# A decoder kernel on one core: GpSimd pauses twice in its hand-ordered summation chain

## The reference

```python
x = x + L0_attn(layernorm(x))          # delta-rule attention, 2 heads, chunks of 64
x = x + L0_xattn(layernorm(x), ctx)    # 16 heads, tanh layers on q, k, v
x = x + L0_ffn(layernorm(x))           # router, top 2 of 4 experts, hidden 512
x = x + L1_attn(layernorm(x))          # causal, shared key and value, 16 heads
x = x + L1_xattn(layernorm(x), ctx)    # causal, 16 heads
x = x + L1_ffn(layernorm(x))           # top 2 of 8 experts, hidden 128
```

## Time and profile before

| | us |
|---|---|
| median of 3 runs (5360.71 to 5361.69) | 5361.09 |
| profiled execution | 5361.46 |
| its span, first to last instruction | 5359.7 |
| PE busy | 4697.3 (88%) |
| PEld busy | 3072.0 (57%) |
| DVE busy | 4119.1 (77%) |
| ACT busy | 2322.5 (43%) |
| POOL busy | 3977.9 (74%) |

### The profile page before, as it was taken

The page is one execution under the profiler, slowest core; times in us unless marked ns, Lnnn a source line. Parts: engine busy times, 40 slices in busy tenths (PEclk is TensorE's granted clock), DMA queues, the critical chain, the costliest instruction groups (busy, mean ns, idle before and its releaser), DMA issues.

```text
span 5359.7 us, 108430 instructions
## 1 busy us (share of the span) xinstructions
PE 4697.3 (88%) x28362; PEld 3072.0 (57%) x28362; DVE 4119.1 (77%) x11313; ACT 2322.5 (43%) x4480; POOL 3977.9 (74%) x12365
## 2 busy tenths in 40 slices
PE   1089999999999999999999999999999999899989
PEld 0065656656565565656556565665656556565655
DVE  8867777777777877787777777777777777777778
ACT  0044444454444444443454544445444444444444
POOL 6688585868858587785858868586895858678585
PEclk7599999999999999999999999999999999999999
DMA  3000000000000000000000000000000000000000
GB/s 90 12 9 9 21 1 25 5 9 21 9 21 1 25 5 9 21 1 29 1 13 17 9 21 1 25 5 9 21 9 21 1 25 6 9 21 6 17 1 17
DMA packets 61911, 78.34 MB, mean 15 GB/s; under 512 B 11168, under 2 KB 53808, under 8 KB 61232
## 3 DMA queue, kind: packets, MB, share of 16 engines
q1 hardware_dynamic: 52784, 62.42, 3.5%
q10 hardware_dynamic: 8448, 8.39, 0.5%
HBM read 45.04 MB, written 8.46 MB: 10 GB/s over the span
## 4 chain that ended last, share of the span: by engine, by line
PE 62%; DVE 22%; issue 8%; ACT 6%; SPq 1%; POOL 1%; DVEq 0%; DMA 0%; ACTq 0%; POOLq 0%
PE bank L1264 7%; PE bank L1297 5%; PE bank L1357 5%; PE bank L1183 5%; PE bank L1169 4%; PE bank L1383 3%; PE bank L1195 3%; PE bank L1217 3%; PE bank L1093 3%; DVE smax L1890 3%; PE bank L1100 3%; DVE arena L1500 2%; PE bank L1282 2%; ACT arena L856 2%; PE bank L1175 2%
## 5 line engine op out<-in xcount | busy, mean ns | idle before, releaser
L1890 DVE TENSOR_REDUCE smax<-bank 128x4 f32<-128x512 f32 x768 | 525.4, 684 | 82.8 <-PE bank L1175 37.7
L843 ACT ACTIVATE arena<-bank 128x512 f32<-128x512 f32 x768 | 455.1, 593 | 249.9 <-PE bank L1183 244.1
L1894 DVE TENSOR_TENSOR arena<-bank,smax 128x512 f32<-128x512 f32 x768 | 531.2, 692 | 26.5
L509 POOL TENSOR_TENSOR arena<-arena 128x1024 f32<-128x1024 f32 x17 | 32.2, 1893 | 664.8 <-DVE y_nat L1622 664.7
L1183 PE MATMUL bank<-ident,arena 128*128 128x128 f32 x3072 | 485.5, 281 | 42.3 <-ACT arena L830 25.0
L1264 PE MATMUL bank<-w,arena 128*128 128x512 f32 x1024 | 498.6, 619 | 14.0 <-DVE arena L1832 14.0
L1169 PE MATMUL bank<-arena 64*128 64x512 f32 x1536 | 441.1, 651 | 64.4 <-ACT arena L867 28.0
L1183 PEld LDWEIGHTS bank<-ident,arena 128*128 128x128 f32 x3072 | 346.6, 141 | 242.9 <-ACT arena L832 82.2
L1297 PE MATMUL bank<-w,arena 128*128 128x256 f32 x2048 | 454.1, 380 | 13.9 <-ACT arena L902 13.9
L830 ACT ACTIVATE arena<-arena,rstd 128x512 f32<-128x512 f32 x512 | 368.2, 719 | 199.9 <-DVE arena L1894 195.8
L648 POOL TENSOR_TENSOR acc_a<-acc_s,arena 128x32 f32<-128x32 f32 x1008 | 273.2, 271 | 225.9 <-DVE gate L2011 103.5
(11 more groups left out here) (437 smaller groups left out, 11925.4 us busy)
## 6 DMA issues: line engine op xcount, KB each, us to landing
arena<-in_x_dram SPq DMA_DIRECT2D x35, 512.0 KB, 3.6
xn_next<-arena SPq DMA_DIRECT2D x17, 512.0 KB, 2.9
arena<-cum_dram SPq DMA_DIRECT2D x17, 512.0 KB, 3.8
arena<-in_ctx_dram SPq DMA_DIRECT2D x16, 512.0 KB, 4.0
out_dram<-arena ACTq DMA_DIRECT2D x16, 512.0 KB, 3.2
xn<-xn_next SPq DMA_DIRECT2D x15, 512.0 KB, 2.9
w<-in_L_ffn_w_dram SPq DMA_DIRECT2D x8, 512.0 KB
w<-in_L_ffn_w_dram SPq DMA_DIRECT2D x1, 1024.0 KB
```

The lines of the kernel that those rows point to most:

```text
L509: operation(*operands).then_inc(sum_step, 1)
L843: act.activation(PT[:, v % 2], bank[3 + v % 2][:, :].rearrange("p (h q) -> p h q", h=QH), ACT.Copy).then_inc(S["pt"], 1)
L1890: dve.tensor_reduce(smax[:, u, :], sc, AX, ALU.max).then_inc(S["s_max"], 1)
L1894: dve.tensor_tensor(Ssb[:, u % 4], sc, smax[:, u, :].unsqueeze(2).broadcast_to([P, QH, P]), ALU.subtract).then_inc(S["s_sub"], 1)
```

## The change

GpSimd's chain had one group of rounds from 25 to 58, and now has three, with a wait ahead of round 27 for the norm's step 39 of this iteration (25 steps of `exact_root_seed` and `exact_root`, 6 of the first quotient, 8 remainders), and a wait ahead of round 42 for `k_rows`. The wait for `x_norm` ahead of round 58 is as it was. The assertion on `run["ref"]` only checks the count while the program is built.

```diff
                 pool.wait_ge(S["g_w"], at(it, "g_w", 1))
-                rounds(ROUTER_ROUND, READ_ROUND)
+                rounds(ROUTER_ROUND, QUOTIENT_ROUND)
+                pool.wait_ge(ref_step, nth(it, REF_STEPS, REF_BEFORE + REST_STEPS))
+                rounds(QUOTIENT_ROUND, MIXED_ROUND)
+                pool.wait_ge(S["k_rows"], at(it, "k_rows", 1))
+                rounds(MIXED_ROUND, READ_ROUND)
                 pool.wait_ge(x_norm, nth(it, 1, 1, 2))
@@
                         for part in range(4):
                             for b in range(2):
                                 exact_rest(0, part, b)
+                        assert run["ref"] == REST_STEPS, run["ref"]
                         key_limit(it, 1)
@@
 ROUTER_ROUND = 25
+QUOTIENT_ROUND = 27
+MIXED_ROUND = 42
 READ_ROUND = 58
+REST_STEPS = 39
```

## The result

The changed kernel took 5394.49 us in the median of six executions (5384.93 to 5410.39) against 5360.9 of the kernel before: a ratio of 1.0066, 95% interval 1.0055 to 1.0077. Forecast were 5354.5 with a range of 5338 to 5371. So it is slower by 34 us, and 23 above the range. One of the six executions of the kernel before took 5819.93 us and counts as slow; the ratio leaves it out. One thing belongs to the result at once: the changed kernel's time is not one number. In a later set of executions, beside others on one chip, its median was 5373.66 (5359.61 to 5395.43, eleven executions; ratio 1.0029, 1.0018 to 1.0039), while the kernel before stayed between 5357.5 and 5364.1 in 25 executions there. The experiments show which iterations are hit in an execution, though not why these. What is said of "after" rests on the first set's profile, with a span of 5391.4.

The account below looks back on a forecast made before the run. The path was taken to run from TensorE through VectorE's remainders back to TensorE, GpSimd's own time being no bound. Per iteration -0.91 + 0.5 = -0.41, times 16 -6.6, giving a median of 5354.5 us, range 5338 to 5371.

Parts of the forecast that it names:

- The gain at the remainders: VectorE's first quotient and eight remainders, freed of GpSimd's company, go from 7.54 to 6.63 us: 0.91 gained per iteration.
- TensorE's cover: TensorE's wait of 1.06 us at expert 2's transposes can take in the 0.91; no more than some 1.06 gainable there.
- The pause and the slip: GpSimd pauses 10.5 us ahead of round 27; its chain ends 8.1 later; au keeps a margin of 3.7, no stall.
- The second wait: GpSimd's wait for the key rows ahead of round 42 is satisfied 3.5 us before it is reached: cost 0.
- What slides in beside VectorE: GpSimd's later centering runs beside VectorE's small steps of the decay's exponential: loss 0.5 to 0.8 per iteration, 0.5 taken.
- rival 2: Chain over 9.3 us late, so the centering's subtraction holds an exponential instruction: +0.85 per iteration, 5375 us; chance 0.13.
- The price of a hold: A small VectorE instruction beside GpSimd's subtraction loses at most 1.35 us, bounded by L1788; 0.1 to 0.4 taken.
- No row shows these steps beside GpSimd: Claim that no profile row had the exponential's small VectorE steps beside GpSimd work, so their loss was estimated from other lines.
- The clock adds no term: TensorE's granted clock is 1.00 (2.4 GHz) in the changed stretch and none of its instructions moves: no cost.
- the +-0.3 of the phase: Allowance in the forecast's own range, 5345 to 5366, for how GpSimd's later rounds meet VectorE's instructions.
- The net -0.41: Sum per iteration: 0.91 gained at the remainders less 0.5 lost beside the exponential; times 16, -6.6 us.
- None of the four: Rivals: kinder phase (chance 0.36), centering holds the exponential (0.13), au too late (0.03), pause does nothing (0.06).

Follow-up runs that it names:

- idle_wait: Changed kernel with its wait for the key rows ahead of round 42 replaced by one for a semaphore satisfied long before; 5370.4 us, ratio 1.0024.
- fill_held: Changed kernel with more TensorE filler products, whose results are unused, in the waits around the latent layer; 5367.9 us, ratio 1.0016.
- held_in_four: Changed kernel without the key-rows wait, with added filler products around the latent layer and GpSimd's centering subtraction cut in four; 5359.2 us, ratio 0.9997.
- second_only: Kernel before plus only the wait for the key rows ahead of round 42, without the pause ahead of round 27; 5410.4 us, ratio 1.0092.

## Why the prediction was wrong, by its steps

**The gain at the remainders: right.** 4.13 for the eight, 6.62 for the stretch against 6.63. By expert 2's layer it is 1.55 (26.48 to 24.93), more than forecast, since small collisions vanished as well: L1643, now L1647, is back at 0.17 from 0.42. TensorE's cover was 1.06 as said: the fillers behind the mixture start 1.06 earlier (56.06 to 55.0 after the gates), and the rest waits again, 1.87 instead of 1.32.

**The pause and the slip: right.** 10.3 for 10.5, 8.3 for 8.1. au is in time, and nothing waits for it.

**The second wait: right,** with 2.2 to spare instead of 3.5; idle_wait, with the same time, bears out that it costs nothing.

**What slides in beside VectorE: the mechanism seen, its size wrong.** The loss at the exponential was taken as 0.5 and measured 1.34 in the mean. It was rival 2, with a chance of 0.13, that named such a hold, and it came in 12 of 16 iterations, but by another way than rival 2 said: the chain was 8.3 late and not 9.3, and the instruction held is one of the first or second group, as VectorE was late; only two iterations have it in the third group. Two errors lie in it. The price of a hold was bounded by 1.35 from a line beside a 2.35 addition, and in the sum taken as 0.1 to 0.4; it is 1.64. The 1.35 is no bound. VectorE's timeline before has that line here:
```profile
1655.38 1.51 DVE L1788 TENSOR_TENSOR parts<-hrs 128x4 f32<-128x4 f32 x1
```
It ends at 1656.89, with the addition (1654.53 + 2.35), so the line lasted for what was left of the addition, 1.50, and the 1.35 is that less its own time: the row shows a hold to the end. Nor does L1424 speak for instructions that stay free: in each of its 32 executions less than 0.1 us was left of the instruction that GpSimd was at when it started. A nearer row was in the trace of before, in the prologue, where the very same steps run beside the very same subtraction on GpSimd (timelines of VectorE and GpSimd before):
```profile
238.66 1.82 DVE L1540 COPY dec_t<-a_row 128x2 f32<-128x2 f32 x1
...
240.72 1.74 DVE L1543 TENSOR_SCALAR dec_t<-dec_t 128x10 f32<-128x10 f32 x1
```
```profile
238.56 1.89 POOL L509 TENSOR_TENSOR arena<-arena,row 128x1024 f32<-128x1024 f32 x1
240.53 1.90 POOL L509 TENSOR_TENSOR arena<-arena 128x1024 f32<-128x1024 f32 x1
```
"No row shows these steps beside GpSimd" was false: the line's maximum of 1743 ns beside a median of 173 would have shown it. The other error is the phase. The subtraction came 143.9 us after round 25 (1810.26 less 1666.41), where 143.6 was forecast. VectorE's second group was forecast 0.91 earlier than before, 142.2 after round 25, and came at 144.0, 0.1 after the subtraction. The clock's loss of 1.6 at the latent layer had put it there. So the two causes are linked: the fall pushed the exponential onto the subtraction. fill_held bears this out, where without the fall the second group is past in time.

**"The clock adds no term": this step failed.** It was argued from the stretch that gets faster, where the granted clock is 1.00, and not from the places behind it where TensorE's waits lie and where the clock already falls in the kernel before, two or three times an iteration. There the shift decides. It costs 1.3 at the latent layer and some 0.4 more in the second attention, averaged over the iterations. Pairs on one chip show it as a cause: the fillers take 12 us back (5379.8 to 5367.9, 5371.0 to 5359.2) and leave the kernel before as it is; and a delay of 1.6 makes a loss of 42 without the change, and of 13 with the fillers.

**Two terms that the sum left out.** It let the 0.91 pass on in full and gave the second attention nothing beyond the +-0.3 of the phase. Of 1.57 won by expert 2's layer, held_in_four, without the latent fall and the long hold, has 1.21 left behind the mixture and 0.76 behind the second attention. The net -0.41 an iteration that was forecast would thus not have come without the clock's fall either: at part 9 it is -0.10, in fill_held 0.00.

**The rivals.** None of the four is what happened: rival 2 had half of it. That the range did not reach far enough has one main reason: each mechanism was priced by itself, and none allowed that a shift could set off another loss larger than itself.

**What stays open.** Why the clock falls in this iteration and not in the next, and so how the loss of 13 to 34 us is made up in each execution. Why a delay of 0.75 vanishes in the kernel before is only half answered: the length of the iteration goes with the interval of the falls, but what makes it keep to that is not shown. Nor is it known which came first in the changed kernel, the fall or the hold: its first iteration has the fall without a long hold, but so has that of the kernel before. And why the second attention is 0.5 longer behind the pause.

## What to carry to other kernels

Where TensorE's granted clock falls somewhere in every iteration, times of edits need not add: before pricing an edit by its own stretch, list all the falls and the waits ahead of them, and reckon with a shift of one or two us moving them. Here removing falls with filler products was worth more (29 and 38 us) than the 15 us that the change itself could have brought. Follow a gain from one fixed point to the next before asking where it went: this one was spent before the next gates. A long instruction of GpSimd costs by what it lands on: look for the longest execution of each neighbouring line, the prologue's too, and cut such an instruction in pieces rather than move it.

## What the runs showed of the hardware

- A small VectorE instruction that starts 0.09 or 0.11 us after a GpSimd subtraction of 1.89 us is held to its end: 1.83 for 0.16 (second_only) and 1.80 for 0.16 (after). Cut into four pieces of 0.61 the whole stretch is 0.8 shorter.
- The granted clock falls to 1.2 GHz behind idle times of TensorE of 1.87 and 1.08 close together in the kernel after, and also behind 1.32 and 1.08, which in the kernel before usually bring no fall: the latent product 3.43 in second_only, 1.95 before. The two waits alone do not decide.
- A delay of up to 0.75 us an iteration cost nothing over 16 iterations (5360.1 against 5360.2), one of 1.6 to 1.7 cost 2.6 each.
- The granted clock's falls at the second gates return after 317.44 us in all 15 intervals of four kernels with different edits, and after 320.85 in all 15 of second_only; the iterations have these lengths in the mean, to 0.25.
- Two kernels with the same order of work on each engine but for two waits, on one chip, scatter very differently: 5357.5 to 5364.1 in 25 executions of the kernel before, 5359.6 to 5395.4 in 11 of the changed one.
